# Turning the attention outputs by transfer as float16 halves instead of on TensorE

## The reference, cut to what matters

```python
xf = gn(x).reshape(B, 256, 4096)
f = Wq @ xf + bq;  g = Wk @ xf + bk;  h = Wv @ xf + bv      # 32, 32 and 256 channels
beta = softmax(f^T g, axis=1)                                # over the first index of 4096 x 4096
x = x + gamma * (h @ beta)
# second layer
y = relu(bn1(w1 @ gn(x) + b1))                               # 32 channels
z = relu(bn2(w2 @ (all 528 products y_i * y_j) + b2))        # 256 channels
x = x + z
```

## Time and profile before

| | |
|---|---|
| median of 3 runs | 2105.32 us (2105.01 to 2105.93) |
| profiled execution, its own time | 2109.38 us |
| its span | 2107.6 us |
| TensorE busy | 2056.0 us, 98% |
| VectorE, ScalarE, GpSimd busy | 1656.5, 1539.2, 1479.8 us |
| granted TensorE clock | 1.000 |

### The profile page before, as it was taken

How to read it: one execution, slowest core, us unless ns; L and a number is a source line. 1 busy time by engine, 2 the same in 40 slices (tenths; PEclk the granted TensorE clock), 3 DMA queues, 4 the chain that set the end, 5 groups by cost and what they waited for, 6 DMA issues and landing times.

```text
span 2107.6 us, 48084 instructions
## 1 busy us (share of the span) xinstructions
PE 2056.0 (98%) x17334; PEld 1611.1 (76%) x17334; DVE 1656.5 (79%) x3617; ACT 1539.2 (73%) x2456; POOL 1479.8 (70%) x2110
## 2 busy tenths in 40 slices
PE   5899999999999999999999999999999999999999
PEld 3688888888877777777877777777787777777854
DVE  8788988778777877878768788777877768777767
ACT  5677777767776777778777787777777777777767
POOL 3265666667677777878768787777867767677766
PEclk9999999999999999999999999999999999999999
DMA  5165778776476788778478678887836767675632
GB/s 190 37 101 103 129 143 143 139 132 113 84 133 122 146 158 150 154 145 156 98 140 140 117 156 142 159 167 139 157 78 134 144 124 140 118 142 94 139 72 81
DMA packets 728269, 271.89 MB, mean 129 GB/s; under 512 B 674240, under 2 KB 681152, under 8 KB 728000
## 3 DMA queue, kind: packets, MB, share of 16 engines
q1 hardware_dynamic: 728032, 268.82, 66.6%
HBM read 77.07 MB, written 19.92 MB: 46 GB/s over the span
## 4 chain that ended last, share of the span: by engine, by line
PE 86%; DVE 5%; POOL 3%; ACT 2%; issue 2%; DMA 1%; SPq 0%; DVEq 0%; ACTq 0%; POOLq 0%
PE acc L1784 19%; PE acc L1772 19%; PE acc L1773 18%; PE tps L1577 5%; PE acc L1577 5%; PE sps L1597 4%; PE acc L1571 3%; PE tps L1648 3%; PE tps L1650 2%; PE acc L1648 1%; POOL kb L1162 1%; PE tps L1612 1%; DVE ks L863 1%; PE tps L1634 1%; POOL xl L1139 1%
## 5 line engine op out<-in xcount | busy, mean ns | idle before, releaser
L1162 POOL TENSOR_TENSOR kb<-ks,kb 128x512 f16<-128x512 f32 x630 | 760.3, 1211 | 412.1 <-DVE kb L891 315.6
L1772 PE MATMUL acc<-hth,kt 128*128 128x257 f16 x2520 | 587.2, 273 | 1.1 <-DMA kt<-kb 1.1
L1773 PE MATMUL acc<-htl,kt 128*128 128x256 f16 x2520 | 586.6, 273 | 0.0
L1333 ACT ACTIVATE ph<-sps,esc 128x512 f16<-128x512 f32 x394 | 269.5, 684 | 339.7 <-PE sps L1597 329.8
L1345 ACT ACTIVATE ks<-ks,kbias,esc 128x512 f32<-128x512 f32 x630 | 498.9, 805 | 0.0
L1784 PE MATMUL acc<-hth,kt 128*128 128x257 f16 x2520 | 385.8, 274 | 0.0
L863 DVE TENSOR_SCALAR_CACHE_REDUCE ks<-acc 128x512 f32<-128x512 f32 x378 | 259.2, 686 | 158.8 <-PE acc L1577 157.0
L1772 PE MATMUL acc<-hth,ph 128*128 128x257 f16 x1576 | 367.3, 274 | 0.0
L1773 PE MATMUL acc<-htl,ph 128*128 128x256 f16 x1576 | 366.9, 273 | 0.0
L1784 PEld LDWEIGHTS acc<-hth,kt 128*128 128x128 f16 x2520 | 247.7, 98 | 100.6
L1772 PEld LDWEIGHTS acc<-hth,kt 128*128 128x128 f16 x2520 | 247.0, 98 | 41.6 <-issue 6.2
(11 more groups left out here) (254 smaller groups left out, 3444.7 us busy)
## 6 DMA issues: line engine op xcount, KB each, us to landing
rt<-turned SPq DMA_DIRECT2D x96, 256.0 KB, 4.9
xt<-x SPq DMA_DIRECT2D x46, 512.0 KB, 4.5
xb<-x SPq DMA_DIRECT2D x32, 512.0 KB, 4.7
out<-zt SPq DMA_DIRECT2D x45, 256.0 KB, 2.7
kt<-kb SPq DMA_TRANSPOSE x630, 3.2
yb<-turned SPq DMA_DIRECT2D x36, 128.0 KB, 2.6
rt<-turned SPq DMA_DIRECT2D x72, 64.0 KB, 2.2
turned<-yb SPq DMA_DIRECT2D x12, 256.0 KB, 2.5
```

Source lines behind the costliest of these rows:

```text
L1162: tt(kb[:, m % KB_RING, 1], ks[:, m % KS_RING], kb[:, m % KB_RING, 0], ALU.subtract).then_inc(kl_ok, 1)
L1333: A(ph[:, v % SLOTS], sps[v % 2][:], ACT.Exp, scale=esc[:]).then_inc(ph_ok, 1)
L1772: mm(bank[:, 0:C + 1], high[:, q], hth[:, c * QT + q], start=(s8 == 0 and q == 0), stop=False)
L1773: mm(bank[:, 0:C], high[:, q], htl[:, c * QT + q], start=False, stop=False)
```

## The change

- For 28 of the 32 chunks (all but the last of each batch, `by_transfer`), ScalarE's division writes a float16 high half into the space of `ot`. VectorE writes the low half next to it at s8 = 5 (`output_low`). SyncE turns both halves of a tile, [128, 512], with a transposing transfer into the new `od` (`turn_output`, at t % 8 = 7).
- VectorE then adds high and low half for each channel half, four operations at t = 9, 10, 12 and 14 (`finish_turned`), and takes the statistics at t = 16 and 17 (`own_stats`).
- TensorE's `transposed` at t = 4 and 7 goes. Waits that stood before it move to t = 9, and the first matmul of a tile waits for the low half of the output two tiles before too.
- The fourth kept step joins `HIGH_BY_ACT`.
- The ring of x has 13 chunks instead of 14. The order and the steps of the early v inputs change (`VORD`, `V_EARLY`), and some statistics of later batches move from t = 9 to 11.

```diff
-HIGH_BY_ACT = (0, 2)
+HIGH_BY_ACT = (0, 2, 3)
-CAST_AT = (None, 3, None, 6, 7)
+CAST_AT = (None, 3, None, None, 7)
-XR = 14
+XR = 13
+        od = sb("od", [P, QT, 2 * H2, P], f16)
+        oth = ot[:].rearrange("p t c -> p (t c)").bitcast(f16).rearrange("p (t e c) -> p t e c", t=QT, e=2)
-        VORD = (4, 0, 5, 1, 6, 2, 3, 7)
+        VORD = (4, 0, 5, 3, 6, 1, 2, 7)
-        V_EARLY = (12, 15, 18, 21)
+        V_EARLY = (11, 15, 19, 26)
-            return b == 0 or (c < XR - NCH if b == 1 else c < 4)
+            return b == 0 or (c < XR - NCH if b == 1 else c < 3)
+        def by_transfer(G):
+            return G % NCH != NCH - 1
+        def transfers_before(G):
+            return G - G // NCH
+        def tiles_lowered(tile):
+            return QT * transfers_before(tile // QT) + (tile % QT + 1 if by_transfer(tile // QT) else 0)
...
+            def turn_output(tile):
+                G, k = divmod(tile, QT)
+                sp.wait_ge(ot_low, tiles_lowered(tile))
+                if transfers_before(G):
+                    sp.wait_ge(own_ok, 2 * H2 * transfers_before(G))
+                sp.dma_start_transpose(od[:, k], oth[:, k].rearrange("p e c -> p (e c)")).then_inc(od_in, 16)
...
+                        if t % NCH == 7 and tile and by_transfer((tile - 1) // QT) and (J or t >= NCH):
+                            turn_output(tile - 1)
...
+            def output_low(tile):
+                k = tile % QT
+                dve.wait_ge(ot_act, tile + 1)
+                V.scalar_tensor_tensor(oth[:, k, 1], acc[tile % 2][:, 0:C], rinv[:, k:k + 1], oth[:, k, 0],
+                                       ALU.mult, ALU.subtract).then_inc(ot_low, 1)
+            def finish_turned(G, e, h):
+                b, J = divmod(G, NCH)
+                if e == h == 0:
+                    dve.wait_ge(od_in, 16 * QT * (transfers_before(G) + 1))
+                    dve.wait_ge(bv_ok, G + 1)
+                if e:
+                    dve.wait_ge(own_ok, 2 * H2 * transfers_before(G) + h + 1)
+                own = xb[:, x_slot(b, J), h].rearrange("p (t q) -> p t q", t=QT)
+                V.scalar_tensor_tensor(own, od[:, :, H2 * e + h], vout[:, h:h + 1], own,
+                                       ALU.mult, ALU.add).then_inc(own_ok, 1)
+            def own_stats(G, h):
+                b, J = divmod(G, NCH)
+                dve.wait_ge(own_ok, 2 * H2 * transfers_before(G) + H2 + h + 1)
+                V.bn_stats(bst[:, h, J], xb[:, x_slot(b, J), h])
...
+                        if s8 == 5 and tile and by_transfer((tile - 1) // QT) and (J or t >= NCH):
+                            output_low(tile - 1)
...
-                        if J and t in (5, 8):
-                            finish(G - 1, (t - 5) // 3, 1)
-                        if J and t in (6, 11):
-                            second_stats(G - 1, (t - 6) // 5, 1)
+                        if J and t in (9, 10, 12, 14):
+                            finish_turned(G - 1, *((0, 0), (0, 1), (1, 0), (1, 1))[(9, 10, 12, 14).index(t)])
+                        if J and t in (16, 17):
+                            own_stats(G - 1, t - 16)
...
             def divide(tile):
                 act.wait_ge(rinv_ok, tile + 1)
-                k = tile % QT
+                k, G = tile % QT, tile // QT
+                if transfers_before(G):
+                    act.wait_ge(od_in, 16 * QT * transfers_before(G))
+                if by_transfer(G):
+                    A(oth[:, k, 0], acc[tile % 2][:, 0:C], ACT.Copy, scale=rinv[:, k:k + 1]).then_inc(ot_act, 1)
+                    return
...
-                        if J and t in (4, 7):
-                            if t == 4 and b and n >= 1:
+                        if J and t == 9:
+                            if b and n >= 1:
                                 pe.wait_ge(y_ok, y_made(n - 1))
...
-                            transposed(G - 1, (t - 4) // 3, 1)
...
                         elif s8 == 0 and tile >= 2:
                             pe.wait_ge(ot_act, tile - 1)
+                            if by_transfer((tile - 2) // QT):
+                                pe.wait_ge(ot_low, tiles_lowered(tile - 2))
```

More of the change, by code:

```diff
@@ L203, in build @@
         rinv_ok = sem("rinv_ok")
-        ot_act = sem("ot_act")
+        ot_act, ot_low, od_in, own_ok = sem("ot_act"), sem("ot_low"), sem("od_in"), sem("own_ok")
         y_mm, y_ok = sem("y_mm"), sem("y_ok")
@@ L285, in build @@
         NEXT_STATS = tuple((J, t) for J, ts in ((0, (8, 11, 15)), (1, (11, 15, 21)), (2, (11, 18))) for t in ts)
-        LATER_STATS = ((2, 27), (3, 2), (3, 9), (3, 18), (3, 25), (4, 2), (4, 9), (4, 18), (4, 25), (5, 2), (5, 9), (5, 18),
+        LATER_STATS = ((2, 27), (3, 2), (3, 11), (3, 18), (3, 25), (4, 2), (4, 11), (4, 18), (4, 25), (5, 2), (5, 11), (5, 18),
                        (6, 22), (6, 29), (7, 4), (7, 11))
@@ L1051, in attend @@
                             normed(("qk", b + 1, 2 * (J - 2)))
-                        if b < LASTB and J == NCH - 1 and t in (13, 16, 19, 22):
-                            normed(("v", b + 1, VORD[(13, 16, 19, 22).index(t)]))
+                        if b < LASTB and J == NCH - 1 and t - 1 in V_EARLY:
+                            normed(("v", b + 1, VORD[V_EARLY.index(t - 1)]))
             project()
@@ L1225, in _ @@
                             low(("qk", b + 1, 2 * (J - 3) + 1))
-                        if t in (14, 17, 20, 23) and b < LASTB and J == NCH - 1:
-                            low(("v", b + 1, VORD[(14, 17, 20, 23).index(t)]))
+                        if t - 2 in V_EARLY and b < LASTB and J == NCH - 1:
+                            low(("v", b + 1, VORD[V_EARLY.index(t - 2)]))
                         if t == 20 and b and 1 <= n < SHARED - 1:
@@ L1456, in attend @@
                             high(("qk", b + 1, 2 * (J - 2)))
-                        if b < LASTB and J == NCH - 1 and t in (12, 15, 18, 21):
-                            high(("v", b + 1, VORD[(12, 15, 18, 21).index(t)]))
+                        if b < LASTB and J == NCH - 1 and t in V_EARLY:
+                            high(("v", b + 1, VORD[V_EARLY.index(t)]))
             act.wait_ge(set_dve, mark["scaled_qkv"])
@@ L1747, in attend @@
                             rest_of_z(n - 2)
-                        if J and t in (4, 7):
-                            if t == 4 and b and n >= 1:
+                        if J and t == 9:
+                            if b and n >= 1:
                                 pe.wait_ge(y_ok, y_made(n - 1))
-                            if t == 4 and b and n >= 2:
+                            if b and n >= 2:
                                 pe.wait_ge(z_ok, 2 * (n - 1))
-                            if t == 4 and b < LASTB and 4 <= J <= 7:
+                            if b < LASTB and 4 <= J <= 7:
                                 pe.wait_ge(qk_lo, qk_made(b + 1, 2 * (J - 4)))
-                            if (b, J, t) == (0, 2, 4):
+                            if (b, J) == (0, 2):
                                 pe.wait_ge(set_dve, mark["part1"])
-                            transposed(G - 1, (t - 4) // 3, 1)
                         if kept(u):
```

## The result

The changed kernel takes 2143.19 us (median of 4 runs, 2140.38 to 2146.28) where the kernel before took 2105.62 beside it: a ratio of 1.0174, interval 1.0158 to 1.0191. It is 37 us slower; 11 us faster was forecast.

The account below looks back on a forecast made before the run. The prediction took TensorE, busy 98% of the span, to bound the kernel. Its terms, 24.1 - 16.0 + 3 = 11.1 us, rounded to 11, took the median of 2105.32 to 2094.3 us, with a range of 2080 to 2111.

Parts of the forecast that it names:

- B: Rival: turned outputs land late, each 1 us later costing TensorE 1 us in each of 21 chunks; chance 0.15.
- D: Rival: ScalarE is late with its 126 added exps, 102 us at worst, 2196 us; chance 0.03.
- TensorE's turns: On TensorE, 56 groups of four turns removed, each worth its full 0.43 us: 24.1 us saved.
- exp by ScalarE: On ScalarE, 126 added exps of 812 ns fit into its waits for scores: 0, bounds 0 to 102.3 us.
- ring of x: One chunk fewer, 5 more loads through the single buffer: nothing, at most some 5 us each.
- place of the finishing ops: VectorE's steps 9 to 14: TensorE stalls 1.35 us in 8 chunks, 0.4 in 13 others; 16.0 us lost.
- the relief: VectorE relieved at steps 5 to 8, second chunks of batches 1 to 3: 0 to about 4 us back, 3 taken.
- output turns in the queue: SyncE's queue: 112 more issues of at most 1.23 us, none in a stretch without pause; hidden, 138 us without cover.
- rival E: TensorE's turns were free, hidden behind something else; chance 0.17 together with the rival that losses eat the gain.
- VectorE's lateness: Replayed chunk: finishing ops at 0.82 us start to start make TensorE wait 0.4 us at piece 12, 0.95 at 17.
- Batch 0 taken as 0: The 7 chunks of batch 0 have no low products in those steps, so no VectorE stall was charged: 0.
- Rival C: Landings 0.4 to 0.7 us late, or finishing ops at 0.96, eat the gain: 2103 to 2109; 0.17 with free turns.

Follow-up runs that it names:

- act_only: The kernel before with only the fourth kept step's high half moved from VectorE's cast to a second ScalarE exp: 2098.27 us, 0.9958.
- ring_only: The kernel before with only the x ring of 13 chunks, the new v input order and steps, and statistics from step 9 to 11: 2115.1 us, 1.0037.
- late_finish: The changed kernel with finishing ops at steps 16, 17, 19, 21, statistics at 24, 25, first tile's output turn at 22: 2117.43 us, 1.0052.
- no_turns: The changed kernel with later finishing ops and statistics, one earlier load, and the 112 output turns left out (output incomplete): 2093.3 us, 0.9933.
- cast_back: The changed kernel with the fourth kept step's high half cast by VectorE again: 2173.0 us, 1.0313.

## Why the prediction was wrong, by its steps

The measured time lies above the stated range of 2080 to 2111 us, where only B and D had put it, and the runs show neither as the cause. The ledger, from the differences of ratios (estimates where an interaction is in them):

| term | forecast, us | shown, us | by |
|---|---|---|---|
| TensorE's turns | -24.1 | -24 (0.4 at 56 places) | starts of steps |
| exp by ScalarE | 0 | -8.8 | act_only |
| ring of x | 0 | +7.8 | ring_only |
| place of the finishing ops, less the relief | +16.0 - 3 | +26 | late_finish |
| output turns in the queue | 0 | +20 | no_turns |
| rest | | +16 | 36.6 less the others |
| sum | -11 | +36.6 | |

**TensorE's turns: right.** 0.43 us a group was the price; 55 of the 56 places show it, and rival E is out. The relief of the second chunks of batches 1 to 3, taken as 3 us, came too: their step 8 is 2.4 us shorter in sum.

**VectorE's lateness: the mechanism right, the term mis-sized, and this is the first step that failed.** The stalls came where they were put, at pieces 12 and 16 to 17. The outputs that rival B feared landed early in the replayed chunk and late in others, and the loss did not go with it. What was wrong is the price from start to start of an op beside GpSimd, 0.82 us, taken from one row at one place. In the trace after, 69 of the 112 finishing ops overlap a GpSimd op on two tensors by more than 0.06 us, and take 1.28 us in the mean; the 43 others take 0.79, and the 29 of them that overlap no GpSimd op at all take 0.74 to 0.75. The old finishing ops, which read PSUM, took 742 ns beside such an op and 743 without. The rule of the Trainium skill that the prediction cited ("SBUF — State Buffer", "SBUF: two separate sides") says this of two inputs in SBUF, and the trace agrees so far that the op beside GpSimd gets longer; by it the change swapped 56 ops that don't contend for 112 that do. GpSimd's own subtraction (L1213) gets longer too, 1.48 us in the mean beside such an op of VectorE and 1.17 else. The cast, with one input, is stretched as well (0.42 us in the mean without such a neighbour and 0.83 with one, on the kernel before), which the rule as the prediction cited it does not say. The range had 0.96 as its end, a mean over ops in other places. And an op that GpSimd stretches also moves those behind it to other neighbours: the product next to it went from 0.84 to 1.56. The replay kept all other durations as they were. In the eight full chunks that made 18.9 us for 10.8, in the 13 others 10.8 for 5.2; late_finish, with the same ops at later steps, brought both to 0.0. The subtraction for the low half went at 0.40 us from start to start, as taken.

**Batch 0 taken as 0: wrong.** It has no low products in those steps, but setup work of the weights and the statistics of three later batches. It lost about 18 us there, 11.0 of them in the chunk of the late load and 6.7 in the six others. That the setup work is what fills VectorE there is read from its list; no run takes it away.

**The ring taken as nothing, at most 5 us a load: wrong.** The single buffer is free only when VectorE has read it, and a late VectorE makes a late load: 9.4 us of waiting for ScalarE, and half a clock for TensorE in part of that stretch.

**ScalarE's exps taken as 0: too little.** The relief of GpSimd was taken as nothing for want of a row, and that of VectorE entered only in its sum of busy time; in act_only, where nothing else changes, GpSimd's wait for VectorE's cast falls from 315.6 us to 156.6. Rival D is out: cast_back is slower, not faster.

**SyncE's queue taken as hidden: wrong, the second large step.** I counted four issues of 1.23 us a chunk, wrote that none falls in a stretch without pause, and asked only whether the output lands in time. The rows of SyncE's queue before the change deny the first for the sixth chunk of batch 2: the queue has hardly a pause there, and an output turn falls in it. What pays is who stands behind: the key turn, then the slot of `kb`, then the high exp, then the exp of a fresh step. The exp by ScalarE had just put a third such op in that line.

**What was to be seen.** Waits near pieces 12 and 17 in batches 1 to 3 were there, the absence of them in batch 0 was not. A finishing op was to take 0.7 to 1.0 us and took 1.09 in the mean. Rival C's price, 0.96 for a finishing op, has the right sign and is too small; no rival joined it with the queue and the ring.

**What stays open.** Some 10 of the 16 us of rest are, in no_turns, in the second, third, sixth and eighth chunk of batch 0, which lose 0.3 to 2.2 us where the turns should bring 0.86; that setup work and late finishing ops meet in steps 21 to 25 there is read from the trace, not tried. Why transfers cost 4 us in one setting and 20 in the other is argued above, not shown. Terms of the ledger measured on different kernels need not add: the exp is worth 9 us on the kernel before and 29 on the changed one.

## What to carry to other kernels

Before work is taken from a full engine, look at the slack of those that receive it in the very steps, with durations from ops that have the same memory and the same neighbours, not from the mean. An issue in an ordered queue costs what waits behind it, so follow each transfer that is moved back one place to the buffer that it frees. An edit's parts should be timed alone: here one of three, the exp, gained 9 us by itself, and the whole lost 37.

## What the runs showed of the hardware

A VectorE op with two inputs in SBUF took 0.73 us alone and up to 1.68 us beside a GpSimd op on two tensors (L944), a cast from SBUF 0.41 to 1.54 us (L915); the old finishing op, with one of its inputs in PSUM, kept its time (742 ns beside such an op, 743 without). A transposing transfer held SyncE's queue for 1.23 us (median) with four blocks of 128x128 float16 and for 1.25 with eight, and landed in 2.6 us or 3.2 us (medians), so four blocks were no cheaper to issue. And the clock of TensorE was granted at 0.57 in the mean from 382.0 to 386.0, behind a gap of 1.99 us in its work, and at 0.50 from 389.0 to 395.5, at and behind a gap of 3.15 us; the kernel before runs the same stretch full, at 1.00.
